# A state-space mixer with routed experts: three PSUM banks in turn for the state inputs, down products in the gate's bank, and new slot tables

## The chip, the cores and the metric
The kernel runs on one core of a Trainium2 chip. The metric is the device time of one execution in microseconds (us); the time shown is a median of runs. The profile and the trace come from one execution.

## The reference
For 32 sequences of 256 tokens with 128 features, all in fp32, one layer is computed: a selective state-space mixer on the normalised input, and then a mixture of experts on the normalised result.

```python
h = causal_conv4(xn @ in_proj_w.T[:, :256]) + conv_b          # 256 channels
u = h
dt = clip(sigmoid(u @ dt_w.T + dt_b), 1e-4, 1.0)
A = -exp(A_log)                                               # 256 x 16
Bm, Cm = u @ B_w.T, u @ C_w.T                                 # 16 states
dA = exp(clip(dt[:, :, None] * A, -5, 5))
dB = dt[:, :, None] * Bm[:, None, :] * u[:, :, None]
state = dA * state + dB + 1e-6                                # over 256 steps
y = sum(state * Cm[:, None, :], -1) + D * u
x = x + (y * silu(z)) @ out_w.T

probs = sigmoid(layernorm(x) @ router_w.T + routing_bias)     # 8 experts, the best 2
shared = (silu(xt @ sg_w.T) * (xt @ su_w.T)) @ sd_w.T
routed = sum over the two of share * (silu(xt @ wg.T) * (xt @ wu.T)) @ wd.T
x = x + shared + routed
```

## The kernel before
**Groups, units, halves.** The 8192 tokens are taken in 16 groups of 512 tokens (two sequences). For each group the scan over time is done for each of the 16 states by itself: that is a unit, and there are 256, numbered j. A unit has two halves of 128 channels. For one unit, GpSimd (`state_input`, L755) or ScalarE (L942) makes dBT, tokens by channels; `KINDS` says which. TensorE turns it by transposes into the PSUM banks `p_db`, channels by 512 tokens (`inputs_by_channel`, L1037, in the tables `i0` and `i1`, for the unit after the slot's). ScalarE makes dA = exp(dt * A) (`decays`, L881, `x`, four units ahead), GpSimd clamps it if need be (`c`). VectorE scans each half in its bank (`scan_state`, L1284, `s0`, `s1`) and multiplies it by C into SBUF (`multiply_states`, L1295, `t0`, `t1`). TensorE adds the 16 products up in `p_y` (`sum_states`, L1053, `h`). There are two `p_db` banks, one for each half. The semaphore `times_c` counts the multiplies, two in each unit; the transposes of half 0 of unit j wait until half 0 of unit j-1 has been multiplied.

**The other work of a group.** It goes through the bank `p_misc` in a fixed order: the transposed input (xnT), the convolution in two halves of two parts (u0, v0, u1, v1), dt (dt0, f0, dt1, f1), B and C (bc, cT), the gate z (z0, z1) and w = dt * u (wT0, wT1) for the group ahead; the turned y (yb0, yb1), the output product (op, L1099), the second norm (xn2T) and the router (logit, rank) for the group behind. ScalarE or VectorE empties each (`empty_misc`). For the first group every other one uses the bank of the down product.

**Experts.** Tokens are scattered to the order of their experts by GpSimd's indirect DMAs (L788, `S`), in batches of two groups, the last two groups alone, and gathered again (L802). Four tiles of 128 tokens make a quad; the shared expert of a group is a quad too. There are 66 quads. Each goes through `gate` (L1202, `G`) into `p_gu`, a bank for each half of the quad, SiLU on ScalarE (L970, `V`), `up` (L1211, `U`) into the same banks, the product on VectorE (L1406, `P`), `down` (L1223, `N`) into the bank `p_dn`, and the emptying: `empty_down` on ScalarE for a routed quad (L978, `E`), `add_shared` on VectorE for a shared one (L1411, `Q`). Weights come by SP's DMAs (`W`), the tiles too (`T`, turned in `X`); `Y` stores, `O` writes the result, `C` adds the gathered rows.

**What sets the order.** Each engine's program is a table of pieces written out by hand, run for each group: `..._FIRST` before group 0, `..._SLOTS` for groups 0 to 15, `..._LAST` after. The n-th time that a name stands in a table is slot n of the group (slot 16k + n in all). `plan` puts each step of a quad into a slot, counted from the slot where the quad starts, by `GATE_LAGS`, `SILU_LAG` and so on. A quad starts every 4 slots (slots 1, 5, 9 and 13 of a group), every 2 in the last 14 slots of the scans (from `END_FROM`), and every slot after `TAIL`, slot 257, where three sets of banks are taken in turn (`bank_sets`): `p_gu`, `p_db` and `p_y`. Every engine works strictly in the order of its table; semaphores join them. Routing is 29 small steps on VectorE (`route`, `r`) for the last group of a batch, with `rank` on TensorE between the 16th and the 17th.

## Time and profile before

| | us |
|---|---|
| median of 3 runs | 1336.18 (1332.47 to 1336.85) |
| the profiled execution | 1334.87 |
| its span, first to last instruction | 1333.1 |
| TensorE busy | 1196.3 (90%) |
| VectorE busy | 1133.8 (85%) |
| ScalarE busy | 899.9 (68%) |
| GpSimd busy | 846.9 (64%) |
| granted TensorE clock, mean | 0.97 |

PE is TensorE's matmuls, PEld its weight loads, DVE VectorE, ACT ScalarE, POOL GpSimd, SP the engine that issues most DMAs. A wait's row gives the engine and line that stood idle, what released it, the total, the number of times and the longest. Matmuls overlap by a part of their length, so a row of eight in the timeline is longer than what it adds to the chain of work.

### The profile page before, as it was taken

How to read it: one execution, taken by the hardware profiler on the slowest of the kernel's cores; microseconds unless marked ns; L12 is line 12 of the kernel's file. 1: busy time of each engine (PE TensorE's matmuls, PEld its weight loads, DVE VectorE, ACT ScalarE, POOL GpSimd, SP SyncE). 2: the span in 40 equal slices, each digit the busy share in tenths (PEclk: the TensorE clock that was granted, in tenths of full speed). 3: DMA queues.
4: the chain of work that ended last, by engine and by line, in shares of the span. 5: the costliest groups of instructions: out<-in, count | busy, mean ns of one | idle time of the engine just before them, and what ended most of it. 6: DMA issues, size and time to landing. Idle time of an engine off the chain costs nothing.

```text
span 1333.1 us, 26551 instructions
## 1 busy us (share of the span) xinstructions
PE 1196.3 (90%) x8725; PEld 1024.6 (77%) x8725; DVE 1133.8 (85%) x1788; ACT 899.9 (68%) x1435; POOL 846.9 (64%) x1370
## 2 busy tenths in 40 slices
PE   6878889799989999999999999999999998888773
PEld 3656767578887888888888888788888987888663
DVE  0899988989898989999898989999999989984232
ACT  4766655658777877779686868778786878653311
POOL 3454453864558874878668874888578875756434
PEclk9899988989999999999999999999999999999887
DMA  6322121235543666356544556255544656666663
GB/s 193 91 73 66 63 67 54 88 109 181 165 156 92 201 194 185 103 169 189 174 130 139 177 184 198 87 187 173 182 121 153 198 159 187 190 208 213 209 206 85
DMA packets 149594, 199.90 MB, mean 150 GB/s; under 512 B 14288, under 2 KB 87888, under 8 KB 149456
## 3 DMA queue, kind: packets, MB, share of 16 engines
q1 hardware_dynamic: 136368, 178.96, 43.4%
q0 software_dynamic: 8192, 16.79, 4.2%
q10 hardware_dynamic: 4896, 2.43, 0.6%
q8 instruction: 72, 1.18, 0.4%
q14 instruction: 66, 0.54, 0.1%
HBM read 169.48 MB, written 28.64 MB: 149 GB/s over the span
## 4 chain that ended last, share of the span: by engine, by line
PE 59%; DVE 19%; issue 8%; ACT 7%; POOL 4%; DMA 2%; POOLq 0%; DVEq 0%; SPq 0%; ACTq 0%
PE p_db L1037 11%; DVE p_db L1284 11%; PE p_y L1053 10%; PE p_misc L1062 8%; PE p_dn L1223 6%; PE p_gu L1211 5%; DVE h L1295 4%; PE p_gu L1202 4%; PE p_misc L1099 2%; PE p_misc L1117 2%; PE p_misc L1073 2%; ACT dA L881 2%; POOL ysel L802 1%; PE p_misc L1152 1%; PE p_misc L1143 1%
## 5 line engine op out<-in xcount | busy, mean ns | idle before, releaser
L1284 DVE TENSOR_TENSOR_SCAN p_db<-dA,p_db 128x512 f32<-128x512 f32 x512 | 617.8, 1218 | 81.3 <-PE p_db L1037 78.6
L755 POOL TENSOR_SCALAR dBT<-wT,bcT 128x256 f32<-128x256 f32 x704 | 337.0, 479 | 254.2 <-ACT wT L916 127.5
L1037 PE MATMUL p_db<-ident,dBT 128*128 128x128 f32 x2048 | 312.5, 278 | 70.8 <-DVE h L1295 61.2
L881 ACT ACTIVATE dA<-dt_sb,A_sb 128x510 f32<-128x510 f32 x512 | 332.8, 711 | 46.8 <-DVE p_db L1284 45.5
L1295 DVE TENSOR_TENSOR h<-p_db,c_wide 128x512 f32<-128x512 f32 x512 | 342.9, 682 | 7.1
L1037 PEld LDWEIGHTS p_db<-ident,dBT 128*128 128x128 f32 x2048 | 238.4, 143 | 124.6 <-issue 98.1
L1053 PE MATMUL p_y<-ident,h 128*128 128x128 f32 x2048 | 270.6, 278 | 0.1
L1053 PEld LDWEIGHTS p_y<-ident,h 128*128 128x128 f32 x2048 | 239.6, 144 | 16.7 <-issue 15.9
L942 ACT ACTIVATE dBT<-wT,eps,bcT 128x256 f32<-128x256 f32 x320 | 165.2, 591 | 0.0
L788 POOL DMA_INDIRECT xs_dram<-xn,slot x128 | 127.0, 993 | 57.6 <-issue 35.2
L802 POOL DMA_INDIRECT ysel<-ys_dram,slot x128 | 123.8, 967 | 62.4 <-issue 33.9
L1062 PE MATMUL p_misc<-xnT,wtap 128*128 128x512 f32 x248 | 116.7, 592 | 0.0
L1211 PE MATMUL p_gu<-xT,wring 128*128 128x128 f32 x648 | 86.6, 277 | 3.7 <-ACT hm L970 3.7
L1223 PE MATMUL p_dn<-wring,hm 128*128 128x128 f32 x648 | 87.3, 279 | 1.5 <-ACT yo L978 1.1
L1202 PE MATMUL p_gu<-xT,wring 128*128 128x128 f32 x648 | 86.7, 278 | 0.7 <-ACT xT L928 0.7
L1211 PEld LDWEIGHTS p_gu<-xT,wring 128*128 128x128 f32 x648 | 78.9, 192 | 10.1 <-ACT hm L970 7.2
L1223 PEld LDWEIGHTS p_dn<-wring,hm 128*128 128x128 f32 x648 | 79.9, 193 | 8.2 <-ACT yo L978 4.2
L1202 PEld LDWEIGHTS p_gu<-xT,wring 128*128 128x128 f32 x648 | 80.8, 195 | 6.7 <-issue 5.8
L1406 DVE TENSOR_TENSOR hm<-p_gu,hm 128x512 f32<-128x512 f32 x116 | 76.1, 659 | 8.3 <-PE p_gu L1211 8.3
L881 ACT ACT_TABLE_LOAD x59 | 75.7, 1283 | 1.0
L970 ACT ACT_TABLE_LOAD x40 | 51.3, 1283 | 29.3 <-PE p_gu L1202 28.9
L970 ACT ACTIVATE hm<-p_gu 128x512 f32<-128x512 f32 x116 | 61.8, 583 | 12.8 <-PE p_gu L1202 12.4
(211 smaller groups left out, 1476.4 us busy)
## 6 DMA issues: line engine op xcount, KB each, us to landing
c_wide<-rows_dram SPq DMA_DIRECT2D x256, 256.0 KB, 4.3
wring<-w_moe_dram SPq DMA_DIRECT2D x169, 384.0 KB, 4.2
xt<-xs_dram SPq DMA_DIRECT2D x41, 256.0 KB, 4.9
ys_dram<-yo SPq DMA_DIRECT2D x34, 256.0 KB, 2.4
dA<-w_moe_dram SPq DMA_DIRECT2D x12, 384.0 KB, 4.2
x_sb<-x_dram SPq DMA_DIRECT2D x16, 256.0 KB, 4.1
out_dram<-x SPq DMA_DIRECT2D x15, 256.0 KB, 2.5
xs_dram<-ysel SPq DMA_DIRECT2D x4, 512.0 KB, 6.0
```

Of the source, the lines that this page charges most:

```text
L755: op = pool.tensor_scalar(dBT[:, j % DBT_RING, c], wT[:, g % 2, c], bcT[:, g % 2, 0, c, n:n + 1], STATE_EPS, ALU.mult, ALU.add)
L802: pool.indirect_dma_start(out=ysel[:, j, c], out_offset=None, in_=ys[b % 2], in_offset=bass.IndirectOffsetOnAxis(ap=slot[:, b % ROUTE_RING ...
L881: act.activation(dst[:, :, 1:], src[:, :, 1:], ACT.Exp, scale=A_sb[:, half, n:n + 1]).then_inc(exp_done, 1)
L942: op = act.activation(dBT[:, j % DBT_RING, c], wT[:, g % 2, c], ACT.Identity, scale=bcT[:, g % 2, 0, c, n:n + 1], bias=eps[:])
L1037: mm = pe.transpose(p_db[half][:, c * P:(c + 1) * P], dBT[:, j % DBT_RING, c, half * P:(half + 1) * P], ident[:])
L1053: mm = pe.matmul(p_y[pair][:, c, half * P:(half + 1) * P], h[:, j % H_RING, half, t0:t0 + P], ident[:], is_transpose=True, start=n == c == ...
L1062: mm = pe.matmul(misc_bank(f"u{half}", g).rearrange("p (s t) -> p s t", s=SPG), wtap[:, t, half * P:(half + 1) * P], xnT[:, :, t:t + SEQ], ...
L1202: mm = pe.matmul(banks[i][:, half, cols], w[:, half * P:(half + 1) * P], tokens, start=True, stop=True)
L1211: mm = pe.matmul(banks[i][:, half, cols], w[:, HID + half * P:HID + (half + 1) * P], tokens, start=True, stop=True)
L1223: mm = pe.matmul(p_dn[:, t], hm_of[BANK_SET[at]][:, i, half, t % 2 * P:(t % 2 + 1) * P], w[:, 2 * HID + half * DM:2 * HID + (half + 1) * D ...
L1284: dve.tensor_tensor_scan(p_db[half][:], dA[:, j % DA_RING, half], p_db[half][:], 0.0, ALU.mult, ALU.add).then_inc(scan_done, 1)
L1295: dve.tensor_tensor(h[:, j % H_RING, half], p_db[half][:], c_wide[:, j % C_RING], ALU.mult).then_inc(times_c, 1)
```

## The change
- There are three `p_db` banks. Half `half` of unit j uses bank (2j + half) mod 3 (`input_bank`), and the transposes wait for the multiply three halves before.
- The bank `p_dn` is gone. A quad that starts before slot 257 puts its down products into `p_gu[0]`, its own gate bank (`down_bank`), and the first half of the next quad's `gate` waits until they are emptied. Later quads put them into `p_db[2]`. At the start, every other piece of the first group uses `p_gu[1]`.
- `up` goes in one slot for both halves (lags 2, 2), `down` too (3, 3), and the emptying comes one slot sooner (3).
- All slot tables are written anew, with the same pieces. Of the tables only those of TensorE, VectorE and ScalarE for the groups 0 to 15 are shown. In the tables before group 0: GpSimd's order of the last pieces is d0 d1 c0 where it was c0 d0 d1; TensorE's is z0 z1 i0 i1 where it was z0 i0 i1 z1; ScalarE's is wT0 wT1 x0 z0 z1 x1 x2 x3 where it was wT0 x0 wT1 x1 x2 x3 z0 z1. In the tables after group 15, for the last batch: VectorE's routing step `slot` stands behind the products of slots 261 and 262, where it stood behind that of 261 alone; between logit and rank TensorE has N259 G260 X261 N260 G261 U261, where it had G260 X260.

```diff
@@ -51,6 +51,7 @@
 COMB_DVE = 4
 DA_RING = 5
 H_RING = 3
+DB_BANKS = 3
 C_RING = 6
 C_LEAD = 3
 DBT_RING = 3
...
 PE_SLOTS = (
-    "h U N yb0 G i0 U i1 h", "N G i0 X G i1 U G U", "yb1 U i0 N h G X xnT h", "i1 u0 i0 N X v0 N i1 op",
-    "i0 h X i1 N u1 G N i0", "X h i1 U U v1 h i0 X", "xn2T G i1 dt0 X f0 h U i0", "dt1 N f1 i1 h logit i0 G N",
-    "X i1 U U i0 X bc N i1", "h G h X i0 G i1 z0 G", "U N N G i0 z1 U cT i1", "U N i0 X G X h rank N",
-    "i1 h X wT0 U i0 wT1 i1 N", "G h G U i0 i1 N h X", "G U X X i0 h i1")
+    "G N i0 U h G yb0 i1 h", "U G i0 xnT X i1 X G yb1", "h U X N i0 N u0 i1 v0", "i0 i1 op U X X h N N",
+    "u1 N i0 U h G X i1 U", "v1 G i0 i1 xn2T N h U logit", "i0 h i1 N dt0 f0 i0 G i1", "X dt1 f1 U h G X i0 U",
+    "U i1 h N N G i0 bc G", "i1 U i0 z0 N X i1 X G", "N z1 h cT G i0 U i1 X", "U G X h i0 rank N U N",
+    "wT0 h i1 G i0 h X X wT1", "U N i1 G i0 h X i1 h", "U h i0 i1 N G X")
 DVE_SLOTS = (
-    "C stats1 Q s0 s1 t0 t1 P s0 s1", "Q Q t0 t1 yd0 Q s0 t0 Q s1", "P yd1 P t1 P s0 t0 P s1 t1",
-    "s0 t0 C s1 t1 C x1 C C Q", "s0 t0 s1 C Q stats2 C P t1 s0", "s1 C t0 t1 s0 C t0 P s1 t1",
-    "s0 P t0 s1 t1 lg s0 r t0 s1", "C Q r P r t1 Q s0 Q r", "t0 r s1 Q r C P t1 r s0", "P r r t0 r s1 r t1 s0 r",
-    "P C t0 r C s1 r P r t1", "r s0 r r Q r r r t0 r", "P s1 r t1 Q r s0 r C r", "s1 t0 t1 C P r Q s0 s1 r",
-    "t0 t1 P C r Q Q")
+    "stats1 P s0 s1 Q t0 t1 s0 yd0 C", "s1 t0 Q t1 s0 C yd1 s1 Q C", "t0 s0 P t1 t0 s1 s0 C t1 P",
+    "C Q C x1 P P t0 C stats2 Q", "P s1 s0 t1 t0 s1 s0 t1 s1 Q", "P t0 lg Q s0 r t1 r t0 r",
+    "r Q r s1 r s0 r t1 s1 t0", "r P t1 P Q r s0 r P s1", "t0 r t1 C r s0 r P t0 s1", "r s0 t1 r s1 r t0 s0 C P",
+    "Q C C t1 P Q C s1 Q t0", "r r C s0 r r r r Q r", "r Q C r r t1 Q t0 s1 r", "s0 t1 s1 C t0 r s0 t1 r C",
+    "P Q s1 P t0 P t1")
 ACT_SLOTS = (
-    "V d V e0 e1 d", "x V x X xnT d", "x d X E V E", "x E E X u0 E", "d x X x V V", "x X u1 X x xn2T",
-    "V X dt0 dt1 E d", "d sig d E V X", "E x x E E x", "X V d bc V d", "x z0 V X E z1", "X cT E V d d", "x V X d V E",
-    "E wT0 E wT1 d X", "d X V x x x", "V E d X X")
+    "d x E e0 V E", "e1 d V x E xnT", "V d E u0 d X", "x x x X X V", "X d E x V X", "X u1 V E X xn2T",
+    "x E sig dt0 V dt1", "V E x V X d", "x E x bc E E", "d d V x z0 E", "X d z1 d V d", "X X cT x V V", "X x E d E d",
+    "wT0 V d X d x", "d E wT1 V x x", "E X V X X")
...
@@ -150,10 +150,10 @@
 END_QUAD = 2
 GATE_LAGS = (0, 1)
 SILU_LAG = 1
-UP_LAGS = (2, 3)
+UP_LAGS = (2, 2)
 PROD_LAGS = (2, 3)
-DOWN_LAGS = (3, 4)
-EVAC_LAG = 4
+DOWN_LAGS = (3, 3)
+EVAC_LAG = 3
 TAIL_LAGS = (0, 0, 1, 1, 2, 2)
 WEIGHT_LEAD = 2
 XT_LEAD = 2
@@ -453,17 +453,16 @@
         yo = sb("yo", [P, 2, 4, DM])
         ysel = sb("ysel", [P, 2, CHUNKS, DM])
 
-        p_db = [pb(f"p_db{i}", [P, TOK]) for i in range(HALVES)]
+        p_db = [pb(f"p_db{i}", [P, TOK]) for i in range(DB_BANKS)]
         p_y = [pb(f"p_y{i}", [P, 2, CH]) for i in range(PAIRS)]
         p_gu = [pb(f"p_gu{i}", [P, 2, 2 * P]) for i in range(2)]
-        p_dn = pb("p_dn", [P, 4, DM])
         p_misc = pb("p_misc", [P, TOK])
         at_start = [misc_at[name, 0] for name, stage in MISC_STAGE.items() if stage == 1]
 
         def misc_bank(name, g):
 
             if misc_at[name, g] in at_start and misc_at[name, g] % 2:
-                return p_dn[:].rearrange("p c d -> p (c d)")
+                return p_gu[1][:].rearrange("p f t -> p (f t)")
             return p_misc[:]
 
         def misc_before(name, g):
@@ -487,6 +486,15 @@
                 return spare[place], spare_loaded[place], 16 * (turn + 1)
             place = (TAIL_TILE + place - SPARE) % W_RING
             return wring[:, place], w_loaded[place], 16 * (len(range(place, TAIL_TILE, W_RING)) + turn + 1)
+
+        def down_bank(at):
+
+            into = p_gu[0][:].rearrange("p f t -> p (f t)") if ORDER[at][0] < TAIL else p_db[2][:]
+            return into.rearrange("p (c d) -> p c d", c=4)
+
+        def input_bank(j, half):
+
+            return p_db[(HALVES * j + half) % DB_BANKS]
 
         gu_banks = [p_gu, [p_db[i][:].rearrange("p (f t) -> p f t", f=2) for i in range(2)], p_y]
         hm_of = [hm[:]] + [wT[:, j].rearrange("p (i f) t -> p i f t", f=2) for j in range(2)]
@@ -975,7 +983,7 @@
                 n = min(4, ROUTED[b] - 4 * q)
                 act.wait_ge(down_in_psum, QUAD["routed", b, q] + 1)
                 at_least(act, ys_stored[at % 2], 16 * (at // 2))
-                act.activation(yo[:, at % 2, 0:n], p_dn[:, 0:n], ACT.Copy).then_inc(dn_emptied, 1)
+                act.activation(yo[:, at % 2, 0:n], down_bank(QUAD["routed", b, q])[:, 0:n], ACT.Copy).then_inc(dn_emptied, 1)
 
             def store_tiles(b, q):
 
@@ -1032,9 +1040,9 @@
 
                 kind = KINDS[j % NS]
                 pe.wait_ge(dbt_by_pool if kind == "p" else dbt_by_act, of_kind(kind, j) + 1)
-                at_least(pe, times_c, 2 * (j - 1) + half + 1)
+                at_least(pe, times_c, HALVES * j + half + 1 - DB_BANKS)
                 for c in range(CHUNKS):
-                    mm = pe.transpose(p_db[half][:, c * P:(c + 1) * P],
+                    mm = pe.transpose(input_bank(j, half)[:, c * P:(c + 1) * P],
                                       dBT[:, j % DBT_RING, c, half * P:(half + 1) * P], ident[:])
                 mm.then_inc(db_by_pe, 1)
 
@@ -1086,7 +1094,7 @@
                 if name == "u0" and g == 0:
                     pe.wait_ge(amin_ready, 1)
                     pe.wait_ge(misc_emptied, misc_at["xnT", 0])
-                    pe.matmul(p_dn[0:1, 0], amin[:], ident[:], start=True, stop=True).then_inc(amin_in_psum, 1)
+                    pe.matmul(p_gu[1][0:1, 0, 0:P], amin[:], ident[:], start=True, stop=True).then_inc(amin_in_psum, 1)
                     pe.wait_ge(tap_ready, TAP_USES)
                 if name == "xnT":
                     pe.wait_ge(xn_ready, g + 1)
@@ -1191,7 +1199,9 @@
                         _, loaded, value = weights_of(ROUTED0[b] + 4 * r + t)
                         pe.wait_ge(loaded, value)
                 banks = gu_banks[BANK_SET[at]]
-                if BEFORE[at] is not None:
+                if BEFORE[at] is not None and i == 0 and ORDER[BEFORE[at]][0] < TAIL:
+                    pe.wait_ge(dn_emptied, BEFORE[at] + 1)
+                elif BEFORE[at] is not None:
                     pe.wait_ge(prod_done, 2 * BEFORE[at] + i + 1)
                 elif BANK_SET[at] == 1:
                     pe.wait_ge(times_c, HALVES * UNITS)
@@ -1220,7 +1230,7 @@
                 for t in range(2 * i, min(2 * i + 2, tiles_of_quad(quad))):
                     w = ws_sb[:] if quad[0] == "shared" else weights_of(ROUTED0[quad[1]] + 4 * quad[2] + t)[0]
                     for half in range(2):
-                        mm = pe.matmul(p_dn[:, t], hm_of[BANK_SET[at]][:, i, half, t % 2 * P:(t % 2 + 1) * P],
+                        mm = pe.matmul(down_bank(at)[:, t], hm_of[BANK_SET[at]][:, i, half, t % 2 * P:(t % 2 + 1) * P],
                                        w[:, 2 * HID + half * DM:2 * HID + (half + 1) * DM],
                                        start=half == 0, stop=half == 1)
                 if i == 1:
@@ -1269,7 +1279,7 @@
             dve.wait_ge(a_ready, 1)
             dve.tensor_reduce(amin[:], A_sb[:].rearrange("p h n -> p (h n)"), AX.X, ALU.min).then_inc(amin_ready, 1)
             dve.wait_ge(amin_in_psum, 1)
-            dve.tensor_reduce(amin_all[:], p_dn[0:1, 0], AX.X, ALU.min).then_inc(flag_ready, 1)
+            dve.tensor_reduce(amin_all[:], p_gu[1][0:1, 0, 0:P], AX.X, ALU.min).then_inc(flag_ready, 1)
             dve.wait_ge(flag_ready, 1)
             dve.tensor_scalar(flag[:], amin_all[:], -CLIP, None, ALU.is_lt).then_inc(flag_ready, 1)
             dve.wait_ge(consts, CONSTS)
@@ -1281,7 +1291,7 @@
                 if half == 0:
                     dve.wait_ge(clamp_done, j + 1)
                 dve.wait_ge(db_by_pe, 2 * j + half + 1)
-                dve.tensor_tensor_scan(p_db[half][:], dA[:, j % DA_RING, half], p_db[half][:], 0.0,
+                dve.tensor_tensor_scan(input_bank(j, half)[:], dA[:, j % DA_RING, half], input_bank(j, half)[:], 0.0,
                                        ALU.mult, ALU.add).then_inc(scan_done, 1)
 
             def multiply_states(j, half):
@@ -1292,7 +1302,7 @@
                 if half == 0:
                     at_least(dve, y_in_psum, PAIRS * (j - H_RING + 1))
                     dve.wait_ge(c_loaded[j % C_RING], 16 * (j // C_RING + 1))
-                dve.tensor_tensor(h[:, j % H_RING, half], p_db[half][:], c_wide[:, j % C_RING], ALU.mult
+                dve.tensor_tensor(h[:, j % H_RING, half], input_bank(j, half)[:], c_wide[:, j % C_RING], ALU.mult
                                   ).then_inc(times_c, 1)
 
             def add_residual(g):
@@ -1408,7 +1418,7 @@
 
             def add_shared(g):
                 dve.wait_ge(down_in_psum, QUAD["shared", g] + 1)
-                dve.tensor_tensor(x1[:, g % X1_RING], p_dn[:], x1[:, g % X1_RING], ALU.add).then_inc(dn_emptied, 1)
+                dve.tensor_tensor(x1[:, g % X1_RING], down_bank(QUAD["shared", g])[:], x1[:, g % X1_RING], ALU.add).then_inc(dn_emptied, 1)
 
             def add_routed(g, j):
```

## Rows read from the trace of the kernel before

**Rows 1.** The page: busy us (share) and instructions; TensorE in 40 slices.

```profile
PE 1196.3 (90%) x8725; PEld 1024.6 (77%) x8725; DVE 1133.8 (85%) x1788; ACT 899.9 (68%) x1435; POOL 846.9 (64%) x1370
...
PE   6878889799989999999999999999999998888773
```

**Rows 2.** Stretches: length, busy PE, PEld, DVE, ACT, POOL; clock, DMA, GB/s.

```profile
0.00:67.00 67.00, 51.22 (x224) 33.89 (x225) 31.66 (x51) 38.95 (x61) 27.98 (x101) 0.90 0.48 141
67.00:267.00 200.00, 164.58 (x1075) 130.53 (x1073) 186.20 (x274) 125.53 (x208) 107.14 (x193) 0.95 0.23 69
267.00:1200.00 933.00, 890.89 (x6761) 775.55 (x6760) 873.49 (x1355) 702.94 (x1109) 647.94 (x1010) 1.00 0.53 164
1200.00:1334.00 134.00, 89.62 (x673) 84.65 (x672) 42.44 (x111) 32.45 (x58) 63.87 (x68) 0.86 0.57 177
```

**Rows 3.** Waits, 67 to 267 us: who waited, for whom; total, times, longest.

```profile
PE p_db L1037 <- DVE h L1295: 28.3, 26, 2.0
...
DVE p_db L1284 <- PE p_db L1037: 9.4, 15, 1.8
```

**Rows 4.** Waits, 267 to 1200 us.

```profile
DVE p_db L1284 <- PE p_db L1037: 46.9, 53, 2.9
...
PE p_db L1037 <- DVE h L1295: 28.2, 42, 1.6
...
PE p_gu L1211 <- ACT hm L970: 3.7, 9, 0.7
```

**Rows 5.** Timeline around 165 us: start, length, engine, line, operation, idle time before it.

```profile
164.34 1.26 DVE L1295 TENSOR_TENSOR h<-p_db,c_wide 128x512 f32<-128x512 f32 x2
...
165.16 0.63 PE L1037 MATMUL p_db<-ident,dBT 128*128 128x128 f32 x4 [1.93 <-DVE h L1295]
```

**Rows 6.** Groups of instructions, 267 to 1200 us: busy, mean ns; idle before, releasers.

```profile
L1284 DVE TENSOR_TENSOR_SCAN p_db<-dA,p_db 128x512 f32<-128x512 f32 x402 | 485.4, 1218 | 48.5 <-PE p_db L1037 46.9 <-issue 0.2
L1295 DVE TENSOR_TENSOR h<-p_db,c_wide 128x512 f32<-128x512 f32 x401 | 268.6, 682 | 5.2
```

**Rows 7.** The chain of work, 633 to 637 us: start, length, what.

```profile
633.06 1.72 PE p_misc L1062 x4
634.78 0.89 PE p_gu L1202 x8
635.67 0.44 PE p_db L1037 x4
636.11 0.87 PE p_y L1053 x8
```

**Rows 8.** Emptying a down product: timeline around 1224 us, and all of line 1411.

```profile
1222.00 2.45 PE L1223 MATMUL p_dn<-wring,hm 128*128 128x128 f32 x16
...
1224.49 0.60 ACT L978 ACTIVATE yo<-p_dn 128x512 f32<-128x512 f32 x1 [7.06 <-PE p_dn L1223]
...
L1411 DVE TENSOR_TENSOR x<-p_dn,x x16: 672/681/692, 161.5 to 1290.7; 128x512 f32<-128x512 f32 x16
```

**Rows 9.** Timeline around dt0, 642 to 647 us, ScalarE and then TensorE.

```profile
642.88 1.09 ACT L970 ACTIVATE hm<-p_gu 128x512 f32<-128x512 f32 x2
643.98 1.28 ACT L897 ACT_TABLE_LOAD   x1
645.28 0.69 ACT L897 ACTIVATE dt_sb<-p_misc,chan_sb 128x512 f32<-128x512 f32 x1
...
642.91 1.02 PE L1073 MATMUL p_misc<-u_sb,wdt_sb 128*128 128x512 f32 x2
...
646.02 1.13 PE L1117 MATMUL p_misc<-u_sb,wdt_sb 128*128 128x512 f32 x2
```

**Rows 10.** Timeline of the start: the first dBT and the first transposes.

```profile
31.54 6.60 POOL L755 TENSOR_SCALAR dBT<-wT,bcT 128x256 f32<-128x256 f32 x12 [3.57 <-ACT wT L916]
...
33.74 1.97 PE L1037 MATMUL p_db<-ident,dBT 128*128 128x128 f32 x8 [3.07 <-POOL dBT L755]
```

**Rows 11.** Timeline, 1252 us: the first scatter of the last batch.

```profile
1252.21 1.04 POOL L788 DMA_INDIRECT xs_dram<-xn,slot  x1 [11.57 <-DVE slot L1391]
```

41 lines of the change are left out of this document (19 added, 22 removed), and 18 rows, old and new, of tables (ACT_FIRST, DVE_FIRST, PE_FIRST).

## The prediction, made before the changed kernel had run

> **What bounds the kernel now.** I read the page's busy times first, then busy time by stretch, then the waits of the two busiest engines in each stretch, then one stall in the timeline. TensorE is busy 90% of the span and VectorE 85%, and both are nearly full over the whole middle [rows 1]. The stretches part the kernel in four [rows 2]. From 267 us, when the experts have joined, to 1200 us TensorE is busy for 890.9 of 933 us and VectorE for 873.5: TensorE sets the pace, and VectorE would take over after only 17 us more. From 67 to 267 us there are few quads, TensorE has 164.6 of 200 us and VectorE 186.2: there VectorE sets the pace. From 1200 us the scans are over and a chain of routing, scatter, experts and gather runs with both engines partly idle. In the middle there is little idle time to be had: 42.1 us of TensorE in 933, and 13.8 us of VectorE in 200.
>
> What it is spent on is one loop between the two engines. TensorE's `inputs_by_channel` waits for VectorE's multiply that frees the bank: 28.2 us in 42 waits of the middle stretch. That leaves 13.9 of the 42.1 us for everything else, 3.7 of it for the experts' SiLU [rows 4]. VectorE's scan waits for these transposes: 46.9 us. In the early stretch the two are 28.3 and 9.4 us [rows 3]. The timeline shows the loop: the two multiplies begin at 164.34, and the transposes behind them start at 165.16, as the first has ended, after 1.93 us of idle time [rows 5]. With two banks, half 0 of unit j+1 can only be turned when half 0 of unit j has been multiplied, and its scan then has as cover what VectorE still has of unit j.
>
> **The change part by part.**
>
> *Third bank.* It adds no instruction. The transposes of a half now wait for the multiply of three halves before, not two. So half 0 of j+1 needs half 1 of j-1, and half 1 of j+1 needs half 0 of j. The bound moves forward by one multiply (0.68 us) where the two multiplies stand together, and by a scan and a multiply (1.9 us) where they alternate [rows 6]. The new tables alternate them: VectorE's order is s1(6) t0(6) s0(7) t1(6) t0(7) s1(7) s0(8), where before it was s0 s1 t0 t1 or s0 t0 s1 t1 of one unit. TensorE's average wait is 28.2/42 = 0.67 us, so the moved bound takes away most of them. Bounds in the middle stretch: 0 and 28.2 us gained. I take 18, two thirds, because VectorE has only 17 us less work than TensorE there [rows 2] and each will still now and then find the other late. In the early stretch VectorE sets the pace, so its idle time counts and TensorE's 28.3 us do not: bounds 0 and 13.8 us, of which 9.4 are waits for these transposes [rows 3]; I take 5.
>
> *Down products in the gate's bank.* The same matmuls write another bank, so they cost nothing themselves. New is that `gate` of the next quad, first half, waits until the down product is emptied. What is queued behind it on TensorE is everything, the transposes for the scans too. What covers it is TensorE's own work between `N` and the next quad's first `G`: i0 and h in the tightest place of a slot table (0.44 + 0.87 = 1.31 us), wT0, h and i1 in the next (0.44 + 0.87 + 0.44 = 1.75 us), and the other two are longer [rows 7]. Emptying takes 0.04 us to start, 0.60 us on ScalarE or 0.68 on VectorE, and some 0.05 us back: 0.7 us in all [rows 8]. So 0.6 us is to spare if ScalarE stands ready. Bounds: 0, and 52 quads x 0.7 = 36 us if the cover were always gone. A gain is excluded, since before the down bank was its own. I take 2, near the low end, since `E` stands just ahead of what ScalarE does next. In the last 14 slots quads come every 2 slots, with the cover i0 (0.44), h, h and i1, and once nothing: 0.26 + 0.7 us, and about 0.2 where the shared quad is emptied behind two routing steps on VectorE. That is 1.2 us at least, 6 x 0.7 = 4 at most; I take 2.
>
> *Shorter lags.* Both halves of `up` and of `down` now go together. On VectorE the add of the shared quad (`Q`) now stands right behind the second product (`P`) where the quad starts in slot 5 of a group, which is so in five groups. There it waits for the second half of the down product, 0.89 us (as 8 matmuls of `gate` [rows 7]), with scans queued behind it. 5 x 1 = 5 us of VectorE at most, 0 if the third bank's lead holds TensorE busy; I take 2.
>
> *ScalarE's order.* Before, SiLU (`V`) comes ahead of dt0 and dt1. Now it stands between them, so in the 11 groups with a quad there the function changes once more. The rows give a switch 1.28 us: the load starts at 643.98, as the SiLU ends at 643.97, and the sigmoid starts at 645.28 [rows 9]. That is 11 x 1.283 = 14 us of an engine that is busy for 703 of 933 us [rows 2]. On TensorE: f0 ends at T, dt0 is emptied at T + 0.04 + 1.28 + 0.69 = T + 2.0. Ahead of dt1 TensorE has i0, G, i1 = 0.44 + 0.89 + 0.44 = 1.77 us, so it stalls 0.3. The SiLU then ends its first half at T + 3.9, and `U` would start at T + 3.8. About 0.4 us x 11 = 5 us, less where `sig` has switched already (six groups). Bounds 0 and 14; I take 3.
> The Trainium skill (ScalarE: Activation LUTs, What ACT_TABLE_LOAD costs) puts a drain of about 1.38 us behind the 1283 ns, 2.66 us for a switch. These rows show the load at its 1.28 us and 0.02 us to the next operation, so they do not show the drain. An estimate by the page's figure would be 29 us of ScalarE in place of 14.
>
> *Start.* Before, the first dBT came at 31.54, waiting for wT, whose second half ScalarE emptied behind the first dA, and the first transposes at 33.74 [rows 10]. Now wT1 is emptied ahead of that dA, and GpSimd does the dBT of units 0 and 1 ahead of the clamp. The first scan can come 1 to 3 us sooner; against that z0 and z1 precede it on TensorE, and the dA of unit 0 comes later by the 0.6 us of an emptying. Bounds -3 and 0; I take -2.
>
> *Tail.* The three sets of banks stay, and the third dB bank replaces the down bank. The scatter of the last batch starts at 1252.21, when `slot` is ready [rows 11]. Before, that step stood behind the products of one quad; now it stands behind those of two, but `rank` is no longer waited for, since matmuls of four quads stand ahead of it. I see no net: bounds -6 and +6, taken as 0.
>
> *The SP queue.* `W`, `T`, `Y` and `c` are moved by a slot or so, and the leads of two slots for weights and six buffers for C stay. TensorE's waits have no row for a weight, so this costs nothing; a late weight would show there.
>
> **Sum.** -2 - 5 - 18 + 3 + 2 + 2 + 2 = -16 us. The profiled execution took 1334.87 us, with a span of 1333.1; that is 1.3 below the median of the runs shown, 1336.18. 1334.87 - 16 = 1318.9, and against the median 1320.
>
> **The rivals.** *All of it is gained* (chance 0.10): nearly all waits for the banks go and no new one comes: 28.2 + 9.4 + 3 = 41 us, so 1296. For it: the bound moves by more than the average wait. Against it: VectorE has only 17 us to spare.
>
> *Nothing changes* (0.15): the bank waits go, and other waits take their place. VectorE then waits for a TensorE that has other work ahead of the transposes, which most of its 46.9 us already are, since TensorE waits for it only 28.2. The gain is then 5 to 13 us in place of 25, the costs above stay 9: 1332 to 1340. This includes the case that the third bank does not do what it says, since TensorE, in order, arrives no sooner.
>
> *Slower by the gate's wait* (0.19): ScalarE is not ready when the down product is. A SiLU with the loads around it holds it for 1.28 + 1.09 + 1.28 = 3.6 us [rows 9]. It decides from the point where the average of 52 quads is (18 + 5 + 2 - 7)/52 = 0.35 us above what I took. At 0.8 us a quad, the cost is 42 us in place of 2, so 1360; at 0.5 it is 26, so 1344. Against it: ScalarE is busy for 703 of 933 us, so it is mostly there in time.
>
> *Slower by the switches* (0.01): each of the two switches around dt0 holds TensorE for its whole load again, 11 x 2 x 1.283 = 28 us in place of 3: 1345. This is where the drain of the Trainium skill's section on ACT_TABLE_LOAD would lead; the rows speak against it [rows 9].
>
> **How the numbers follow.** The forecast case, 1308 to 1331, has 0.55. Faster by over 0.3% (4 us, about what a measurement of this kernel can tell from no change), that is below 1332, holds the forecast and the first rival: 0.65. Within 0.3%: 0.15. Slower: 0.20. The range leaves out 2 in 10: the best half of the first rival at 1303, and the slower cases above 1341.
>
> **What would show it.** Right: in the waits of 267 to 1200 us, TensorE's row for VectorE's multiply falls from 28.2 to under 10, VectorE's row for the transposes falls below 30, and the stretch from the 67 us to the last scan shortens by some 20 us. The gate's wait shows as TensorE waiting for `yo` or `x`: under 5 us. Wrong: over 20 us there; or VectorE's waits stay at 45 while TensorE's go; or TensorE waits at `up` and dt1 for ScalarE by over 10 us.

## The result, and the profile after

The changed kernel takes 1297.3 us (median; 1294.7 to 1300.2) beside 1334.3 for the kernel before on the same chip: a ratio of 0.9726, with a 95% interval of 0.9691 to 0.9761. That is 37 us gained where 16 were forecast, and below the range's lower end of 1303. The profiled execution has a span of 1296.3 us.

The page of the kernel after, engines' busy times and TensorE's slices (before: [rows 1]):

```profile
PE 1179.1 (91%) x8725; PEld 1016.8 (78%) x8725; DVE 1095.9 (85%) x1788; ACT 909.0 (70%) x1446; POOL 845.4 (65%) x1370
...
PE   7879897899999999999999999999999997987763
```

VectorE has the same 1788 instructions and 37.9 us less busy time. The prediction had no term for that: it treated VectorE's work as fixed and only its idle time as something to win. TensorE too is busy for 17.2 us less with the same 8725 matmuls.

The last three stretches of [rows 2], with its columns. The last two meet at 1170 us here, 6 us behind the start of the last scan, and at 1200 us in the kernel before, 7.5 us ahead of it:

```profile
67.00:267.00 200.00, 176.96 (x1201) 140.88 (x1200) 197.16 (x301) 139.46 (x231) 121.95 (x219) 0.98 0.29 86
267.00:1170.00 903.00, 872.04 (x6711) 767.16 (x6710) 831.49 (x1337) 705.07 (x1109) 639.41 (x988) 1.00 0.54 167
1170.00:1297.00 127.00, 77.87 (x589) 73.54 (x587) 34.37 (x99) 26.44 (x49) 52.35 (x57) 0.83 0.56 177
```

From 67 to 267 us VectorE now gets 301 instructions done in place of 274 and is busy for 197 of 200 us. In the middle TensorE is busy for 872.0 us and VectorE for 831.5: the distance between the two has grown from 17 to 41 us. The clock granted to TensorE from 67 to 267 us was 0.98, where it was 0.95 [rows 2].

Waits of the kernel after, 67 to 267 us (VectorE's row for the transposes, 9.4 us in [rows 3], is gone):

```profile
PE p_db L1045 <- DVE h L1305: 14.0, 24, 1.3
```

Waits of the kernel after, 267 to 1164 us, the start of the last scan (before: [rows 4]; `p_gu <- yo` is the gate's new wait, `x <- p_gu L1233` the shared quad's add):

```profile
DVE p_db L1294 <- PE p_db L1045: 27.7, 26, 2.0
...
DVE x L1421 <- PE p_gu L1233: 16.9, 5, 3.4
...
PE p_db L1045 <- DVE h L1305: 12.3, 21, 1.7
```

```profile
PE p_gu L1212 <- ACT yo L986: 1.0, 1, 1.0
```

From 267 us on, the bank waits fell from 28.2 to 12.3 us and from 46.9 to 27.7. The gate waits once. The add waits up to 3.4 us in each of five groups, not 1.

Where the time went shows when one sets the starts of the same scan side by side (start of the first scan of each group of 16 units, worked out from the two traces):

```
scan of unit    before   after   gained by then   in the group
0                 35.0    32.2        2.7
16                98.3    93.8        4.5          group 0    1.8
32               166.7   155.2       11.5          group 1    6.9
48               242.3   221.6       20.7          group 2    9.1
64               313.4   286.1       27.3          group 3    6.6
224             1051.1  1010.8       40.3          groups 4-13  13.0
255 (last half) 1207.5  1164.1       43.4          groups 14-15  3.1
end             1333.1  1296.3       36.8          behind it  -6.6
```

Of groups 4 to 13, the even ones, in which the routing of a batch of two groups is done, fell from 76.5 to 73.8 us each. The odd ones took 71.0 and now take 71.2. So the 36.8 us are 2.7 at the start, 24.6 in groups 0 to 3, 13.0 in groups 4 to 13 (all of it in the even ones), 3.1 in the last two groups, and a loss of 6.6 behind the last scan.

### The profile page after: what moved, and what is told of

It is laid out like the page before. It is cut to its first block, busy times and chain, and to the rows that moved or that the text cites. A ratio compares the mean times of both kernels' runs of the same rounds, so it can differ in the third digit from the quotient of the medians.

```text
span 1296.3 us, 26561 instructions
## 1 busy us (share of the span) xinstructions
PE 1179.1 (91%) x8725; PEld 1016.8 (78%) x8725; DVE 1095.9 (85%) x1788; ACT 909.0 (70%) x1446; POOL 845.4 (65%) x1370
## 4 chain that ended last, share of the span: by engine, by line
PE 56%; POOL 15%; DVE 14%; issue 9%; ACT 5%; DMA 1%; POOLq 0%; SPq 0%; DVEq 0%; ACTq 0%
PE p_db L1045 10%; PE p_y L1061 9%; PE p_misc L1070 7%; DVE p_db L1294 7%; PE p_gu L1221 5%; PE p_gu L1233 5%; PE p_gu L1212 4%; POOL ysel L810 4%; POOL dBT L763 4%; DVE h L1305 4%; POOL xs_dram L796 3%; PE p_misc L1107 2%; ACT dA L889 1%; PE p_misc L1175 1%; PE p_db L1233 1%
## 5 line engine op out<-in xcount | busy, mean ns | idle before, releaser
L889 ACT ACTIVATE dA<-dt_sb,A_sb 128x510 f32<-128x510 f32 x512 | 332.1, 710 | 11.8 <-DVE p_db L1294 10.7
L1305 DVE TENSOR_TENSOR h<-p_db,c_wide 128x512 f32<-128x512 f32 x512 | 337.5, 676 | 1.3
L1045 PE MATMUL p_db<-ident,dBT 128*128 128x128 f32 x2048 | 301.6, 276 | 37.3 <-DVE h L1305 28.2
L1061 PEld LDWEIGHTS p_y<-ident,h 128*128 128x128 f32 x2048 | 235.4, 142 | 12.5 <-issue 10.1
L1212 PE MATMUL p_gu<-xT,wring 128*128 128x128 f32 x648 | 85.8, 276 | 2.5 <-ACT xT L936 1.5
L1212 PEld LDWEIGHTS p_gu<-xT,wring 128*128 128x128 f32 x648 | 79.0, 192 | 6.1 <-issue 4.2
L1233 PE MATMUL p_gu<-wring,hm 128*128 128x128 f32 x632 | 79.5, 277 | 4.2 <-DVE hm L1416 4.2
L1221 PE MATMUL p_gu<-xT,wring 128*128 128x128 f32 x648 | 80.5, 278 | 1.0 <-ACT hm L978 1.0
L1221 PEld LDWEIGHTS p_gu<-xT,wring 128*128 128x128 f32 x648 | 77.0, 194 | 4.6 <-ACT hm L978 3.1
L1233 PEld LDWEIGHTS p_gu<-wring,hm 128*128 128x128 f32 x632 | 74.2, 192 | 5.7 <-DVE hm L1416 2.8
L901 ACT ACTIVATE u_sb<-p_misc,chan_sb 128x512 f32<-128x512 f32 x31 | 21.3, 686 | 74.2 <-PE p_misc L1070 74.2
L1070 PEld LDWEIGHTS p_misc<-xnT,wtap 128*128 128x128 f32 x248 | 42.1, 189 | 31.8 <-issue 30.6
```

The costliest lines, as they stand in the source:

```text
L889: act.activation(dst[:, :, 1:], src[:, :, 1:], ACT.Exp, scale=A_sb[:, half, n:n + 1]).then_inc(exp_done, 1)
L1045: mm = pe.transpose(input_bank(j, half)[:, c * P:(c + 1) * P], dBT[:, j % DBT_RING, c, half * P:(half + 1) * P], ident[:])
L1061: mm = pe.matmul(p_y[pair][:, c, half * P:(half + 1) * P], h[:, j % H_RING, half, t0:t0 + P], ident[:], is_transpose=True, start=n == c == ...
L1070: mm = pe.matmul(misc_bank(f"u{half}", g).rearrange("p (s t) -> p s t", s=SPG), wtap[:, t, half * P:(half + 1) * P], xnT[:, :, t:t + SEQ], ...
L1212: mm = pe.matmul(banks[i][:, half, cols], w[:, half * P:(half + 1) * P], tokens, start=True, stop=True)
L1221: mm = pe.matmul(banks[i][:, half, cols], w[:, HID + half * P:HID + (half + 1) * P], tokens, start=True, stop=True)
```

## The experiments

Ratios are to the kernel before on the same chip, with 95% intervals. "Before" and "changed" name the kernel that an edit starts from. All of them compute everything.

### Is the third bank needed, or the order of the pieces?

**Changed, with two banks.** Same tables, the waits as before:

```
-            return p_db[(HALVES * j + half) % DB_BANKS]
+            return p_db[half]
-                at_least(pe, times_c, HALVES * j + half + 1 - DB_BANKS)
+                at_least(pe, times_c, HALVES * (j - 1) + half + 1)
```

> The changed kernel with two banks for the state inputs again: half 0 and half 1 of every unit use their own bank, and the transposes wait for the multiply two halves before. All tables stay. If the third bank carries the gain, VectorE now meets a scan right behind the multiply that frees its bank (t0 of unit 6, then s0 of unit 7), with no work between for the 0.63 us of the transposes and two handovers: some 0.7 us in each unit, up to 180 us, of which part is hidden: 1380 us or more. If the new order of the tables carries it and the bank is only along, the time stays within 10 us of 1297.

Measured: 1711.9 us, 1.2805 [1.2757, 1.2853]. Waits of the whole kernel:

```profile
PE p_db L1045 <- DVE h L1305: 357.4, 288, 3.7
DVE p_db L1294 <- PE p_db L1045: 282.2, 344, 16.4
```

The new order cannot do without the bank: in s1(6) t0(6) s0(7), VectorE asks for half 0 of unit 7 right behind the multiply that frees its bank, and stands while TensorE fills it.

**Before, with the third bank and its own order.** The banks and lags of the change under the old tables. Pieces move only where a lag demands it: some of ScalarE's `E` and `V`, and one shared add (`Q`), which stands two places earlier:

```
-        p_db = [pb(f"p_db{i}", [P, TOK]) for i in range(HALVES)]
+        p_db = [pb(f"p_db{i}", [P, TOK]) for i in range(DB_BANKS)]
-        p_dn = pb("p_dn", [P, 4, DM])
-                at_least(pe, times_c, 2 * (j - 1) + half + 1)
+                at_least(pe, times_c, HALVES * j + half + 1 - DB_BANKS)
```

> The kernel before with its tables and lags, but with three banks for the state inputs and the down products in the gate's bank. What this needs is moved: ScalarE's emptying of slots 0, 1 and 5 stands ahead of the SiLU of slots 2 and 4, the SiLU of slots 13 and 15 behind the emptying, and VectorE's add of slot 7 behind the next first multiply. VectorE keeps its 207 multiplies right behind their own scan. If the bank by itself gives what idle time it takes away, groups 0 to 3 gain the 14.6 us of VectorE's idle time that went there, and the rest some 8: 1312 to 1318 us. If the bank is worth something only together with the new order of VectorE, 1330 us or more.

Measured: 1360.5 us, 1.0187 [1.0154, 1.022]. Slower than before. Groups 0 to 2 gain 9.2 us (207.3 to 198.1). Then the odd groups go from 71.0 to 76.4. Waits of TensorE, whole kernel (L1230 is `gate`, L1063 the transposes):

```profile
PE p_db L1063 <- DVE h L1323: 23.8, 31, 1.7
PE p_gu L1230 <- DVE x L1439: 23.3, 7, 4.0
...
PE p_gu L1230 <- ACT yo L1004: 12.8, 15, 1.4
```

The bank waits fall from 61.2 to 23.8 us and the gate's wait takes 36 us in their place. Of these, 23.3 us are for VectorE's shared add and 12.8 for ScalarE's emptying. This is the rival of the gate's wait, at its price, in the old order.

**Changed, with the emptying of the down product later on ScalarE.** `E` of slot 0 stands two pieces later, behind the emptying of the first y bank and a SiLU, and `E` of slots 1, 4 and 8 one piece later:

> The changed kernel; ScalarE empties the down product later: in slot 0 behind the emptying of the first y bank, in slots 4 and 8 behind the next dA (two of 0.71 us). This makes the rival of the gate's wait happen on purpose. By the covers of the prediction, slots 4 and 8 still fit (2.0 us against 5.2 and 2.2), and slot 0 does not: the first y bank is ready 0.9 us after the down product, then 0.6 and 0.7 us, against a cover of 1.31: 0.9 us a group in 12 groups, so 1308 us. If the gate's wait is not what TensorE meets there, within 3 us of 1297.

```
-    "d x E e0 V E", "e1 d V x E xnT", ...
+    "d x e0 V E e1 E d V x",
```

Measured: 1309.3 us, 0.9799 [0.9766, 0.9833], as expected. The gate's row rises from 1.0 us, once, to:

```profile
PE p_gu L1219 <- ACT yo L993: 12.0, 14, 1.0
```

So 10 to 12 us of the gain rest on ScalarE standing ready at `E` (by the ratios and by the times). The prediction's 2 us for the gate holds only with `E` where the change puts it.

### VectorE's neighbours

On VectorE a multiply right behind the scan that it uses starts after that scan has ended. With anything else between them neighbours overlap. Timeline of VectorE, start and length: first the changed kernel, then the kernel of the next experiment.

```profile
118.85 1.22 DVE L1294 TENSOR_TENSOR_SCAN p_db<-dA,p_db 128x512 f32<-128x512 f32 x1
119.97 0.67 DVE L1305 TENSOR_TENSOR h<-p_db,c_wide 128x512 f32<-128x512 f32 x1
```

```profile
120.39 1.22 DVE L1304 TENSOR_TENSOR_SCAN p_db<-dA,p_db 128x512 f32<-128x512 f32 x1
121.64 0.69 DVE L1315 TENSOR_TENSOR h<-p_db,c_wide 128x512 f32<-128x512 f32 x1
```

In the first the multiply starts 0.10 us before the scan's end, in the second 0.03 behind it. Over each whole trace the median gaps are -0.091 and +0.034 us, that is 0.125 us for each such pair. The kernel before has 207 of them and the changed one 8: 199 x 0.125 = 25 us of VectorE's busy time.

**Changed, with every multiply behind its own scan.**

```
-    "stats1 P s0 s1 Q t0 t1 s0 yd0 C", "s1 t0 Q t1 s0 C yd1 s1 Q C", ...
+    "stats1 P Q s0 t0 s1 t1 yd0 C s0",
+    "t0 Q s1 t1 C yd1 Q C s0 t0",
```

> The changed kernel with three banks; in VectorE's table for groups 0 to 15 each scan is moved to stand right ahead of its own multiply. In the trace of before, 207 multiplies stood right behind their own scan and began 0.034 us after its end; where other work stood between, neighbours overlapped by 0.09 us. The changed kernel has 8 such pairs. If this is a second source of the gain, beside the bank, some 480 pairs now cost 0.125 us each, 60 us of VectorE: in groups 0 to 3, where VectorE sets the pace, 16 us come back, in the rest less: 1315 to 1325 us. If only the bank counts, within 4 us of 1297.

Measured: 1387.8 us, 1.0386 [1.035, 1.0421], far slower than expected. In groups 0 to 2 the price is the one of the pairs: VectorE's busy time rises by 12.6 us, and 94 more pairs x 0.125 make 11.8. In the middle another thing is added: TensorE waits for the multiplies, whole kernel

```profile
PE p_db L1055 <- DVE h L1315: 77.2, 129, 2.3
```

in place of 28.2, since the moved scans put the multiplies at other times than TensorE's table expects. Some 10.8 us more of VectorE's time are the meetings with GpSimd described below, which this order runs into: `weight<-top,share` took 0.78 to 1.21 us 13 times, in place of 0.17.

**Before, with s0 s1 ahead of t0** (two banks, each s1 set ahead of its t0, so no own pair):

> The kernel before, two banks, with VectorE's table for groups 0 to 15 in the order s0 s1 t0 t1 for every unit, so that no multiply stands right behind its own scan. If the pairs cost 0.125 us each by themselves, 25 us of VectorE go and groups 0 to 3 gain 6 us: 1326 to 1331 us. If with two banks the order s0 t0 s1 t1 was needed as cover for the transposes, the gain is eaten: the next scan of half 0 then has only one multiply of 0.68 us as cover for 0.63 us of transposes and two handovers, and the time is 1334 to 1350 us.

Measured: 1411.3 us, 1.0579 [1.0549, 1.0609]. Whole kernel (78.6 and 61.2 before):

```profile
DVE p_db L1294 <- PE p_db L1047: 163.8, 196, 19.1
...
PE p_db L1047 <- DVE h L1305: 113.6, 161, 2.7
```

With two banks the own pair is what the order needs: the early multiply frees the bank. The pair's 0.125 us was the price of two banks, and only the third bank makes it avoidable.

**Before, three banks and s0 s1 ahead of t0** (both edits together):

> As b_three_banks, and with VectorE's order s0 s1 t0 t1 for every unit. If bank and pairs are two sources that the changed kernel joins, this gains 6 to 12 us over b_three_banks: 1303 to 1310 us. If the pairs are hidden, it equals b_three_banks within 4 us.

Measured: 1365.2 us, 1.0217 [1.0184, 1.025], within 5 us of the three banks alone. In groups 0 to 2 VectorE's busy time falls by 4.8 us against them, and its idle time rises by 4.6. The saved time is there, and idle time takes its place, with TensorE's table unchanged.

**Changed, with the shared add later.** `Q` behind the next unit's two scans and first multiply, where it waited 3.4 us:

> The changed kernel; in VectorE's table the add of the shared quad in slot 8 stands four pieces later, behind the next two scans and a multiply. It stood right behind the second product and waited 16.9 us in 5 times for the down product. If this wait holds the odd groups (71.2 us each, no faster than before), they fall to 69.5 and the time by 5 to 8 us, to 1290. If TensorE sets the pace there all the same (busy for 69.1 of 71.2 us), 0 to 2 us.

```
-    ... "r P t1 P Q r s0 r P s1", "t0 r t1 C r s0 r P t0 s1", ...
+    "r P t1 P r s0 r P s1 t0",
+    "Q r t1 C r s0 r P t0 s1",
```

Measured: 1309.2 us, 0.9797 [0.9764, 0.983]. Both views missed. The 16.9 us of waiting are gone from VectorE and the odd groups stay at 70.7 to 71.8, within 0.6 us of the 71.2. In groups 5 and 7 TensorE now waits 2.8 and 2.3 us for GpSimd's dBT, where it waited 0.4 and 0.3. So taking VectorE's wait away hardly shortens the odd groups. In the changed kernel TensorE is busy for 69.1 of their 71.2 us, which points to it as their limit, but no run shows that alone. The even groups get 1 to 3 us longer from group 6 on, with TensorE's wait for GpSimd's dBT up from 6.6 us:

```profile
DVE p_db L1304 <- PE p_db L1055: 63.8, 48, 16.6
...
PE p_db L1055 <- POOL dBT L773: 18.6, 8, 3.2
```

Why the even groups suffer from an edit that acts in the odd ones was followed only to this late dBT.

### GpSimd's order

In the changed table GpSimd's two last scatters of a group stand ahead of the first two dBT of the next group. In the old table one dBT stands ahead of them. As this dBT waits for `wT`, GpSimd stands, and the scatters wait behind it.

**Changed, with one dBT ahead of the two last scatters, as before has it.**

```
-    ... "w0 w1 c C S", "c C S S d", "C d")
+    "w0 w1 c C S c C d S S",
+    "C d")
```

> The changed kernel; of the two dBT that were moved ahead of the scatters of slots 14 and 15 in the experiment that cost 38 us, only the first is moved, as the kernel before has it. If the wait for wT ahead of the scatters is what costs, it costs here too: 1320 to 1332 us. If it was the second dBT or the place behind the last comb alone, within 5 us of 1298.

Measured: 1327.2 us, 0.9939 [0.9916, 0.9961], as expected. Group 3 takes 70.5 us in place of 64.5. From group 5 on the even ones take 75.6 to 76.9 in place of 73.8, the odd ones 73.0 in place of 71.2. GpSimd and TensorE, whole kernel (30.5 and 6.6 in the changed kernel; 127.5 and 6.1 in the one before):

```profile
POOL dBT L769 <- ACT wT L930: 119.6, 11, 12.5
```

```profile
PE p_db L1051 <- POOL dBT L769: 22.0, 13, 6.3
```

**Changed, with both behind the dBT** (and the tail tables of before):

> The same with GpSimd's scatters of slots 14 and 15 behind the dBT of the next group's units 0 and 1. In the changed kernel GpSimd waits in each even group for the routing's slots, 7.8 us in one of them, with these two dBT queued behind. If TensorE needs them sooner (it waits 4.3 us for GpSimd's dBT in all), 2 to 4 us are gained: 1289. If not, equal within 2 us; and if the scatters then reach the next gathers late, 2 to 5 us slower.

Measured: 1331.9 us, 0.9964 [0.9943, 0.9986]; a loss of 38 us against the changed kernel with the same tail tables (1294.0), where at most 5 were expected. The same row for `wT` is back at 119.5 us. Some 30 to 38 us of the change hang on where two scatters stand, and this decides group 3.

**Changed, with GpSimd's whole table of before.**

> The changed kernel with GpSimd's table of before for groups 0 to 15. If GpSimd's order is a third source of the gain, beside the bank and VectorE's order, the middle loses 15 to 35 us: 1312 to 1332. If it matters only at the scatters, this equals the run with one dBT moved within 3 us. If GpSimd's order is free, 1297.

Measured: 1382.6 us, 1.036 [1.0315, 1.0405]. Larger than either view: the norm that GpSimd makes for TensorE is late as well.

```profile
PE p_misc L1119 <- POOL xn L703: 46.7, 16, 5.8
DVE logit L1325 <- PE p_misc L1130: 42.7, 15, 6.6
```

**Before, with the scatters ahead of the dBT**, the counterpart:

> The kernel before; in GpSimd's table the scatters (or gathers) of slots 14 and 15 stand ahead of the dBT of the next group's first unit, where they stood behind it. In the kernel before GpSimd waits 12.7 us in every even group, with this dBT at the head of its queue, until wT is emptied. If the changed kernel's gain in the even groups (76.5 to 73.8 us) comes from filling this wait with the scatters, the even groups fall below 75 here and the time by 10 to 16 us, to 1318 to 1325. If it comes from the banks, it stays within 4 us of 1334.

Measured: 1373.0 us, 1.0272 [1.0226, 1.0318], slower instead of faster:

```profile
POOL xs_dram L794 <- DVE slot L1397: 121.3, 9, 15.2
...
PE p_db L1043 <- POOL dBT L761: 41.0, 13, 7.4
```

In the kernel before, VectorE's routing gives `slot` only near the group's end. A scatter placed early then stands up to 15.2 us with the dBT queued behind it. The changed kernel starts the routing steps about two slots sooner, and there the same wait is at most 9.9 us up to the last scan, and at most 7.9 from 267 us on. Order on GpSimd and order on VectorE are one edit.

### A meeting of VectorE and GpSimd

The trace of the kernel before holds two rows, once in each even group from group 4 on, that the prediction did not read. Timeline, VectorE:

```profile
365.24 1.10 DVE L1346 TENSOR_TENSOR key<-rest,top 128x64 f32<-128x64 f32 x1
366.38 1.19 DVE L1349 TENSOR_TENSOR key<-key,rank 128x64 f32<-128x64 f32 x1
```

and GpSimd at the same time, two operations:

```profile
365.00 2.49 POOL L769 TENSOR_TENSOR w_sb<-dt_sb,u_sb 128x512 f32<-128x512 f32 x2
```

In the changed kernel these two steps take 0.2 us in all the even groups. All 13 long ones of the kernel before (twelve of 1.1 to 1.2 us, and one of 0.75 in group 2) began within `w_sb`'s products and ended 0.08 us behind the one that they met; in sum they hold VectorE for 11.8 us. The changed kernel has none over 0.4 us. The Trainium skill (SBUF — State Buffer, Who interferes with whom) says that a VectorE operation with two inputs in SBUF contends with a GpSimd operation that reads SBUF, that the ports which the two share are an exclusive lock, and that the order of issue decides who is blocked. These rows agree: the product had started first, and VectorE's step ended behind it.

With the 25 us of the pairs these 11.8 account for nearly all of the 37.9 us that left VectorE's busy time. Smaller meetings of the same kind make up more: an estimate from the rows that are longer than others of their form is 4 us before (two steps of the last batch, of 1.00 and 0.86 us at 1188 and 1190 us, beside GpSimd's `x<-x,ysel`, and short ones beside dBT) and under 1 us after.

**Before, with these two steps ahead of a scan and a product** instead of behind them, 1.1 us sooner against `w_sb`'s product:

```
-    ... "t0 r s1 Q r C P t1 r s0", "P r r t0 r s1 r t1 s0 r",
+    ... "t0 r s1 Q r C P t1 r r", "r s0 P t0 r s1 r t1 s0 r",
```

> Kernel before with one edit in VectorE's table: the routing steps key<-rest,top and key<-key,rank (128x64, both inputs in SBUF) stand ahead of the scan s0 of their place instead of behind it. In the trace of before they start at 365.24 and 366.38 and take 1.10 and 1.19 us instead of 0.2, both ending with GpSimd's w_sb<-dt_sb,u_sb (365.00 to 367.49); so in each of the six even groups from group 4 on VectorE loses 1.88 us. One us earlier they lie clear of it. Theory 1 (VectorE's small operations are held by GpSimd's, and VectorE sets the pace there): these two rows fall to 0.2 us each, VectorE's busy time by about 11 us, the even groups from 76.5 to 74.6 us, the kernel to 1322 to 1326. Rival (TensorE sets the pace in the even groups, the held time hides behind it): rows fall, groups stay at 76.5, kernel within 3 us of before. Rival 2 (the long rows have another cause than GpSimd): the rows stay at 1.1 us, time as before.

Measured: 1326.4 us, 0.9922 [0.9898, 0.9947]. The even groups go from 76.5 to 75.0 us and the odd ones stay at 71.0. The steps, shortest, median and longest in ns:

```profile
L1346 DVE TENSOR_TENSOR key<-rest,top x9: 191/224/226, 217.6 to 1233.8; 128x64 f32<-128x64 f32 x7, 128x32 f32<-128x32 f32 x2
```

```profile
L1349 DVE TENSOR_TENSOR key<-key,rank x18: 181/214/1290, 211.4 to 1234.0; 128x64 f32<-128x64 f32 x14, 128x32 f32<-128x32 f32 x4
```

(180/1102/1110 and 181/214/1194 before.) The one of 1290 ns is in group 2, where the edit runs into a meeting. From group 4 on neither step is over 0.23 us. So the held time was on the path: 10 us for two table entries, 1.5 of the 1.9 us in each even group. Two entries of the kernel before, moved, are worth a quarter of the whole change.

**Changed, with one such meeting put in**: `w_sb`'s first half 6 us sooner, in GpSimd's idle time.

```
-    ... "clip0 S c C S", "C d d C d", "c c S C S", "S clip1 d C c", "w0 w1 c C S", ...
+    ... clip0 S c C S C d w0 d C d c c S C S S clip1 d C c w1 c C S ...
```

> Changed kernel with one edit in GpSimd's table: w_sb's first half is made about 6 us earlier, in 3.4 us of GpSimd's idle time between two dBT, where VectorE's routing step hit<-key,win (128x64, both inputs in SBUF, 0.21 us) starts at the same moment. Theory 1: that row takes about 1.0 to 1.3 us in the groups with routing, VectorE's busy time grows by 5 to 7 us, the even groups by 0.5 to 1 us each, the kernel by 3 to 6 us to 1300 to 1304. Rival (hidden behind TensorE): the row is long, the time stays within 1 us of 1298. Rival 2 (GpSimd is not the cause): the row stays at 0.21.

Measured: 1306.5 us, 0.9769 [0.9747, 0.979]: 6 to 8 us lost by the two ratios of the changed kernel (0.9726 and 0.9712), somewhat more than expected. The step named in the expectation was met just as it began and was held in one group of seven. The next one, `win<-top`, was held in six:

```profile
331.91 0.64 DVE L1370 TENSOR_TENSOR win<-top 128x8 f32<-128x8 f32 x1
```

in place of 0.16, together 3.4 us. The rest of the loss goes with another wait, though the two were not told apart: TensorE's for dBT went from 6.6 to 15.2 us, as the product now stands ahead of a dBT.

### The tail

**Changed, with the tail tables of before** (the five `_LAST` tables), and once more beside a repeat of the changed kernel:

```
-PE_LAST = ("X h U X N", "U G yb0 X yb1", ...
+PE_LAST = ("N U h X yb0", "yb1 G G X N", ...
```

> The changed kernel with the tables of before for the stretch after group 15. In the changed kernel the last gather starts 116.7 us after the last scan, before it was 110.1. If the new tail tables cost this, the time falls by 5 to 7 us, to 1291. If it comes from elsewhere (the bank of the tail's down products, work left over from the scans), it stays within 2 us of 1297.

> The changed kernel as it is, to stand beside the next two on the same chip: 1297 us, ratio to before 0.972.

> The changed kernel with the tail tables of before, again: it took 1292.5 us. If the tail tables are the cause, it is 4 to 6 us below the changed kernel in the same hour too; if that was the spread between two calls, they are equal within 2 us.

Measured: 1292.5 us, 0.9672 [0.964, 0.9705]; again 1294.0, 0.9684 [0.9663, 0.9704], beside 1298.4, 0.9712 [0.9686, 0.9737], for the changed kernel. The last batch's first scatter, changed kernel and then this one:

```profile
1214.49 1.11 POOL L796 DMA_INDIRECT xs_dram<-xn,slot  x1 [25.93 <-DVE slot L1401]
```

```profile
1208.93 1.11 POOL L796 DMA_INDIRECT xs_dram<-xn,slot  x1 [16.35 <-DVE slot L1401]
```

The last scans start at 1164.1 and 1163.4, so the scatter comes 50.4 and 45.5 us behind them (44.7 before). By the times, 4.4 and 4.8 us of the loss of 6.6 come with the new tail tables, which place the routing steps behind more products. Of all kernels run this is the fastest, and it beats both of the comparison.

## Why the prediction was wrong, point by point

**Right.** *What bounds the kernel* and the loop between the two engines: its waits fell, VectorE's as said (46.9 to 27.7, "below 30") and TensorE's nearly so (28.2 to 12.3, "under 10"). From 67 us to the last scan 41 us were gained, and not some 20. *The gate's wait*: 1.0 us, under the 2 taken, and its rival was rightly put at ScalarE's readiness: with `E` later it costs 10 to 12 us, with the old tables 36 (23.3 of them for VectorE's add). *The start*: -2.7 for -2. *The switches of ScalarE*: the 11 extra loads are there (1446 instructions for 1435), ScalarE's busy time rose by 9 us, and no wait of TensorE for dt1 shows, so 3 us were too much. Nor does the drain behind a load show that the page of the Trainium skill (ScalarE: Activation LUTs, What ACT_TABLE_LOAD costs) would add.

**The step that failed is the bound by VectorE's idle time, in the early stretch.** The term was -5, with a bound of 13.8: "VectorE sets the pace, so its idle time counts". Between the scans at 66 and 265 us of the kernel before, 19 us were gained. The bound was no bound, as it holds VectorE's busy time fixed. In groups 0 to 2 that fell from 191.2 to 183.4 us, by 7.8. The own pairs are the part of it that is shown: there are 50 in these groups before and 2 after, so 48 x 0.125 = 6.0 us, and experiments that remove or add them moved it by 4.8 in the old tables and by 12.6 in the new. VectorE's idle time fell by 10.2 as well, from 16.1 to 5.9. One rival was not tested: in group 2 TensorE's busy time fell from 64.3 to 58.2 us, and from 200 to 300 us the granted clock was 0.91 before and 1.00 after. How much of the gain in groups 2 and 3 comes with the clock is open.

**The middle was mis-sized too, for want of a term.** From the scan at 265 us to the last one, 22 us were gained where the net forecast was -18 + 3 + 2 + 2 + 2 = -9. Some 6 of these 22 are in group 3, 13 in groups 4 to 13 and 3 in the last two. The sum had no term for GpSimd's table. Yet group 3 goes by it: one dBT more ahead of the scatters gives back 6.0 of its 6.6 us, and the old place of the scatters costs some 30 us in all. Nor did it have one for the steps that GpSimd holds. The -18 were said to come from the banks, all over the stretch. Summed by group, TensorE's waits for the bank were 3.0 us in each even group of 4 to 13 and 0.2 to 0.8 in each odd one, and are now 0 and 1.4 to 1.6. So the odd groups had nothing to give, and the even ones gave 2.7 us each as their 3.0 went. In the kernel before with the two held steps moved, the 3.0 are 1.6 and the group is 1.5 us shorter: about half of the bank waits there came from steps that GpSimd held, and not from the number of banks. What the bank and what the earlier routing did to the other 1.6 was not told apart. That groups 4 to 13 alone gave 13.0, close to the net of 11 that the terms for the slot tables make (-18 + 3 + 2 + 2), is luck.

**The add `Q`** was put at 1 us in five groups and waited 3.4, 16.9 in all. It cost next to nothing: with the wait gone, the odd groups were 0.5 us shorter at the most. A size was off, in a term that did not count.

**The tail** was taken at 0 within -6 and +6 and lost 6.6: the edge of the bound. The step "`rank` is no longer waited for" weighed less than the products ahead of `slot`.

**The rivals.** The time of "all of it is gained", 1296, was met, but not its story: its sum took the bank waits and the start and nothing else, and 12.3 of its 28.2 us stayed. Time that vanished from VectorE's work, and GpSimd's order, made good for them. That the number fits is luck. The argument used against it ("VectorE has only 17 us to spare") was wrong for the same reason: the change widened that margin to 41 us.

**What is joint and what is single.** The experiments don't add up to the gain, and no sum of parts should be made of them: bank alone +27 us, order of scans alone +77, both +31, GpSimd's scatters alone +38, the changed kernel less its bank +415, less its GpSimd table +85. Only the two held steps came out of the kernel before by themselves. The rest was seen only as one gain, of tables fitted to each other.

## What to carry to other kernels

An engine's busy time is a term of the sum too: before bounding a gain by idle time, look for rows of one form whose durations differ (here 0.2 and 1.1 us) and for neighbours that cannot overlap (0.125 us each, 207 times). Where several engines run by hand-written orders, read a stretch's limit group by group, and don't expect a bank or a moved piece to pay until the other queues are arranged for it. A piece that waits is paid by what is queued behind it: two scatters on GpSimd were worth some 30 us.
